# Routed experts' sums: gathered rows times diagonal matrices of the weights on TensorE, in place of one weighted addition per row on VectorE

## The reference

```python
# third block: 32 experts of inner width 96, 4 of them for each token, and a shared expert
probs = softmax(x @ router_w)
topk_w, topk_idx = top_k(probs, 4);  topk_w = topk_w / sum(topk_w)
eo[t, e] = (silu(x[t] @ w_gate[e]) * (x[t] @ w_up[e])) @ w_down[e]
routed[t] = sum over the 4 chosen e of topk_w[t, e] * eo[t, e]
out = routed + (silu(x @ sh_gate) * (x @ sh_up)) @ sh_down * sigmoid(x @ sh_gate_w)

# fourth block: 16 experts of inner width 256, 2 for each token, with biases
y[t] = sum over the 2 chosen e of gates[t, e] * ((silu(x[t] @ W1[e] + b1[e]) * (x[t] @ W11[e] + b11[e])) @ W2[e] + b2[e])
z = a shared expert of inner width 512;  out = y + z
```

## Time and profile before

| | |
|---|---|
| median of 3 runs | 1688.22 us (1686.22 to 1691.62) |
| profiled execution | 1694.55 us, its span 1692.7 us |
| PE busy | 1260.5 us (74%), 7110 instructions |
| DVE busy | 1250.0 us (74%), 4139 instructions |
| ACT busy | 910.8 us (54%) |
| POOL busy | 412.5 us (24%), 578 instructions |
| line 2151, gathers (POOL) | 96 of 977 ns mean, 93.8 us |
| granted TensorE clock, mean | 0.856 |

### The profile page before, as it was taken

How to read it: one execution, slowest core, us unless ns; L and a number is a source line. 1 busy time by engine, 2 the same in 40 slices (tenths; PEclk the granted TensorE clock), 3 DMA queues, 4 the chain that set the end, 5 groups by cost and what they waited for, 6 DMA issues and landing times.

```text
span 1692.7 us, 24051 instructions
## 1 busy us (share of the span) xinstructions
PE 1260.5 (74%) x7110; PEld 675.0 (40%) x7198; DVE 1250.0 (74%) x4139; ACT 910.8 (54%) x2172; POOL 412.5 (24%) x578
## 2 busy tenths in 40 slices
PE   6988979887422333246678999977899888999976
PEld 2444544444111111131135656513366344666621
DVE  5998979989789999868656566667766865555672
ACT  3898988887254444411344565544444444455454
POOL 0111202002000000003556345265310153232160
PEclk7999989999755555555789999978899999999998
DMA  3010100100293000012332566333211026547220
GB/s 114 26 68 8 49 27 26 55 0 1 80 330 116 3 9 11 1 39 90 114 99 83 180 186 191 100 86 67 55 32 31 35 79 159 158 123 179 98 69 21
DMA packets 141387, 135.41 MB, mean 80 GB/s; under 512 B 75218, under 2 KB 114455, under 8 KB 141203
## 3 DMA queue, kind: packets, MB, share of 16 engines
q1 hardware_dynamic: 126185, 101.99, 20.6%
q0 software_dynamic: 13440, 31.48, 6.1%
q10 hardware_dynamic: 1632, 0.39, 0.1%
HBM read 95.96 MB, written 47.27 MB: 85 GB/s over the span
## 4 chain that ended last, share of the span: by engine, by line
PE 45%; DVE 33%; ACT 9%; issue 8%; another core or an unknown queue 2%; DMA 2%; SPq 1%; POOL 0%; DVEq 0%; ACTq 0%
PE PS L577 40%; DVE RA L1733 6%; DVE nmx L1488 5%; DVE RA L1737 4%; PE PS L573 4%; DVE RA L1291 3%; DVE RA L1294 2%; ACT RA L1879 1%; ACT RA L1929 1%; DVE RB L1291 1%; DVE RB L1294 1%; DVE X L1475 1%; DVE Otok L1218 1%; ACT RB L1885 1%
## 5 line engine op out<-in xcount | busy, mean ns | idle before, releaser
L577 PE MATMUL PS<-RA 128*128 128x512 bf16 (+6 forms) x1961 | 508.3, 352 | 102.4 <-DVE nmx L1488 64.6
L1488 DVE TENSOR_REDUCE nmx<-PS 128x1 f32<-128x512 f32 x512 | 347.2, 686 | 237.2 <-PE PS L577 210.0
L1929 ACT ACTIVATE RA<-PS 128x512 f32<-128x512 f32 x512 | 301.1, 599 | 214.9 <-PE PS L577 151.4
L577 PEld LDWEIGHTS PS<-RA 128*128 128x128 bf16 (+4 forms) x2048 | 200.7, 121 | 356.3 <-issue 142.1
L577 PE MATMUL PS<-RA,Vs 128*32 128x512 f32 x1240 | 204.1, 654 | 5.1 <-ACT RA L1929 1.0
L2055 ACT ACTIVATE RA<-RA 128x8 f32<-128x8 f32 x511 | 107.5, 210 | 143.0 <-DVE RA L1733 142.7
L573 PE MATMUL PS<-ident,RB 128*128 128x128 f32 (+2 forms) x331 | 62.7, 334 | 158.5 <-DVE RB L1666 142.9
L1908 ACT ACTIVATE RA<-PS 128x256 f32<-128x256 f32 (+1 forms) x144 | 55.0, 382 | 171.7 <-PE PS L577 158.3
L1291 DVE TENSOR_SCALAR RA<-PS 128x1024 f32<-128x1024 f32 x96 | 117.0, 1219 | 20.9 <-PE PS L577 20.6
L1879 ACT ACTIVATE RA<-RA,nm 128x512 f32<-128x512 f32 x192 | 128.8, 725 | 0.9 <-POOL nm L2225 0.7
L1294 DVE CUSTOM_DVE_ANT_0 RA<-RA,RB 128x512 f32<-128x512 f32 x192 | 125.1, 689 | 3.3
(11 more groups left out here) (312 smaller groups left out, 2127.1 us busy)
## 6 DMA issues: line engine op xcount, KB each, us to landing
RA<-scr SPq DMA_DIRECT2D x288, 96.0 KB
RA<-wd SPq DMA_DIRECT2D x28, 384.0 KB
xd<-Otok SPq DMA_DIRECT2D x36, 256.0 KB, 3.3
RA<-xd POOLq DMA_DIRECT2D x72, 128.0 KB, 3.8
RA<-wd SPq DMA_DIRECT2D x56, 160.0 KB
RB<-wd SPq DMA_DIRECT2D x20, 384.0 KB
RB<-wd SPq DMA_DIRECT2D x40, 160.0 KB
scr<-parts SPq DMA_DIRECT2D x48, 128.0 KB
```

The costliest lines, as they stand in the source:

```text
L577: return e.matmul(o, l, r, start=first, stop=last)
L1488: e.tensor_reduce(nmx[:, (g + lx) % 3, c:c + 1], bank[(6, 0)[i % 2]], AX.X, ALU.max, negate=True).then_inc(*ROWMAX.up(layer, n, i))
L1929: e.activation(chunk(layer, k, i), bank[(1, 5)[i % 2]], ACT.Exp).then_inc(*EXP.up(layer, k, i))
```

## The change

`gather_steps` now lists three tasks. `gather` i goes through 8 tiles (`XY`, in the place of `XG`), and from the ninth on waits for the merge of the tile to which row i - 8 belonged. `weight` i, three steps later, is a new operation of POOL: the 128x128 identity times the column WJ[:, n, j], which gives a diagonal matrix in one of 8 tiles `DG`. `merge` n, one step after the last `weight` of the tile, is on PE: k float32 matmuls, each a diagonal matrix times a gathered tile, summed in 128 columns of bank 3 or 4, whichever of them no expert item holds (`MERGE_BANK`). DVE then adds the bank to X[n], once per token tile: 16 additions per block in place of 64 and 32. Waits that named an addition of a row name the merge or its addition. By the planner, the merges stand in quarters 194 to 257 and 477 to 508, and `READY3` becomes 208, 224, 241 and 295.

```diff
     XG = RA[:, 8448:9984].rearrange("p (u t k) -> p u t k", u=6, t=2)
+    XY = RA[:, 8448:9472].rearrange("p (u k) -> p u k", u=8)
+    DG = [x[:, i:i + 128] for x, a in ((RA, 9472), (RB, 6272)) for i in range(a, a + 512, 128)]
...
-    GATH = [loads(f"gather{i}") for i in range(6)]
+    GATH = [loads(f"gather{i}") for i in range(8)]
...
     def gather_steps(lx):
-        pairs = 16 * topk[lx]
-        return [([("combine", i - 6)] if i >= 6 else []) + ([("gather", i)] if i < pairs else []) for i in range(pairs + 6)]
+        m, pairs = topk[lx], 16 * topk[lx]
+        steps = []
+        for i in range(pairs + 4):
+            steps.append([("gather", i)] if i < pairs else [])
+            if i >= 3 and i - 3 < pairs:
+                steps[-1].append(("weight", i - 3))
+            if i >= 4 and (i - 4) % m == m - 1:
+                steps[-1].append(("merge", (i - 4) // m))
+        return steps
...
+    MERGE_BANK, held = {}, set()
+    for q in range(4 * (LEAD + STEPS)):
+        for layer, m in ((2, q // 4), (3, q // 4 - LEAD)):
+            for name, i, *_ in plan[layer].get((m, q % 4), ()):
+                if name == "hidden":
+                    held.add(3 + i % 2)
+                elif name == "gated":
+                    held.discard(3 + i % 2)
+                elif name == "merge":
+                    MERGE_BANK[layer - 2, i] = next(bk for bk in (3 + i % 2, 4 - i % 2) if bk not in held)
...
# PE
+            elif name == "merge":
+                n, m = task[1], topk[lx]
+                bk = MERGE_BANK[lx, n]
+                claim(bk)
+                for i in range(m * n, m * n + m):
+                    pe.wait_ge(GATH[i % 8], lx, i)
+                    pe.wait_ge(DIAG, lx, i)
+                    ins = mm(bank[bk][:, 0:128], DG[i % 8], XY[:, i % 8, :], i == m * n, i == m * n + m - 1)
+                ins.then_inc(*MERGE.up(lx, n))
+                free[bk] = [(XW, "routed", lx, n)]
...
# DVE
-            elif name == "combine":
-                i = task[1]
-                n, j = i // topk[lx], i % topk[lx]
-                dve.wait_ge(GATH[i % 6], lx, i)
+            elif name == "merge":
+                n = task[1]
+                dve.wait_ge(MERGE, lx, n)
                 x_last(n)
-                dve.wait_ge(ROUTE, "done", lx)
-                e.scalar_tensor_tensor(out=X[:, n, :], in0=XG[:, i % 6 // 2, i % 2, :], scalar=WJ[:, n, j:j + 1], in1=X[:, n, :],
-                                       op0=ALU.mult, op1=ALU.add).then_inc(*XW.up("routed", lx, i))
-                written[n] = ("routed", lx, i)
+                e.tensor_tensor(X[:, n, :], bank[MERGE_BANK[lx, n]][:, 0:128], X[:, n, :], ALU.add).then_inc(*XW.up("routed", lx, n))
+                written[n] = ("routed", lx, n)
...
# POOL
-                if i >= 6:
-                    pool.wait_ge(XW, "routed", lx, i - 6)
-                e.indirect_dma_start(XG[:, i % 6 // 2, i % 2, :], None, yd[lx],
-                                     bass.IndirectOffsetOnAxis(ap=IDX[:, n, j:j + 1], axis=0)).then_inc(*GATH[i % 6].up(lx, i))
+                if i >= 8:
+                    pool.wait_ge(MERGE, lx, (i - 8) // k)
+                e.indirect_dma_start(XY[:, i % 8, :], None, yd[lx],
+                                     bass.IndirectOffsetOnAxis(ap=IDX[:, n, j:j + 1], axis=0)).then_inc(*GATH[i % 8].up(lx, i))
+            elif name == "weight":
+                i = task[1]
+                n, j = i // k, i % k
+                pool.wait_ge(ROUTE, "done", lx)
+                if i >= 8:
+                    pool.wait_ge(MERGE, lx, (i - 8) // k)
+                e.tensor_scalar(DG[i % 8], ident[:, :], WJ[:, n, j:j + 1], None, ALU.mult).then_inc(*DIAG.up(lx, i))
```

More of the change, by code:

```diff
@@ L256, in build @@
     YOUT = [loads(f"yout{i}") for i in range(6)]
-    GATH = [loads(f"gather{i}") for i in range(6)]
+    GATH = [loads(f"gather{i}") for i in range(8)]
     STORE = loads("store")
     XT_P, SCORE, TURN, VALUE, MISC = (signal("pe_" + n) for n in ("xt", "score", "turn", "value", "misc"))
-    FF_P, GATE_P, HID, XTURN, DOWN = (signal("pe_" + n) for n in ("ff", "gate", "hid", "xturn", "down"))
+    FF_P, GATE_P, HID, XTURN, DOWN, MERGE = (signal("pe_" + n) for n in ("ff", "gate", "hid", "xturn", "down", "merge"))
     LN, XT_V, CLIP, ROWMAX, MISC_V, PARTS_V, FIN, XW = (signal("dve_" + n) for n in ("ln", "xt", "clip", "rowmax", "misc", "parts", "fin", "x"))
@@ L268, in build @@
     XG_A, YO_A = signal("act_xg"), signal("act_yo")
-    ROOT = signal("pool_root")
+    ROOT, DIAG = signal("pool_root"), signal("pool_diag")
     SET, PARTS_P, BIAS_P, NEGMAX = signal("pool_set"), signal("pool_parts"), signal("pool_bias"), signal("pool_negmax")
@@ L412, in build @@
     assert spread(2, gather_steps(0), last + 4, 0.95) <= 4 * STEPS
-    added = [max(4 * n + i for (n, i), tasks in plan[2].items() for t in tasks if t[0] == "combine" and t[1] // 16 == b) for b in range(4)]
+    added = [max(4 * n + i for (n, i), tasks in plan[2].items() for t in tasks if t[0] == "merge" and t[1] // 4 == b) for b in range(4)]
     READY3 = [max(added[b], 4 * (16 * b + 25) + 2, 4 * (48 + LAG) - 9) + 1 for b in range(4)]
@@ L447, in both @@
                     early_step(*task)
+    MERGE_BANK, held = {}, set()
[8 more added lines that the diff above has]
+                    MERGE_BANK[layer - 2, i] = next(bk for bk in (3 + i % 2, 4 - i % 2) if bk not in held)
+        for task in early.get(q, ()):
+            if task[:2] == ("values", 0):
+                (held.add, held.discard)[task[2] // 3](3)
     between, narrow, wide = {}, {}, {}
@@ L2165, in first_rows @@
             if lx:
-                pool.wait_ge(XW, "routed", 0, 16 * topk[0] - 1)
+                pool.wait_ge(MERGE, 0, NT - 1)
             for u in range(6):
@@ L2475, in sp_program @@
             sp.wait_ge(XW, "shared", 1, 8 * b + 7)
-            sp.wait_ge(XW, "routed", 1, 8 * b + 7)
+            sp.wait_ge(XW, "routed", 1, 4 * b + 3)
             e.dma_start(out[b].rearrange("(n p) d -> p n d", p=128), X[:, 4 * b:4 * b + 4, :]).then_inc(*STORE.up("all"))
```

## The result

The changed kernel took 1718.12 us (median of 5 runs, 1715.54 to 1723.19), the kernel before 1688.22 us (5 runs, 1684.98 to 1691.62): 1.0168 of its time, 95% interval 1.0149 to 1.0188. I had forecast 1686.0. It is slower, outside my range, and by the rival to which I had given 4 in 100: POOL is the bound.

A forecast was written before the change was run, and what follows sets the result against it. Neither PE (45% of the chain) nor DVE (33%) alone was taken to bound it. Terms -4.5 + 0.8 + 0.3 + 1.2 = -2.2 us took the median from 1688.22 to 1686.0 us; range 1676 to 1698.

The forecast's parts named there:

- POOL is the bound: Rival, both gather stretches: at 0.85 us per diagonal a pair takes 2.01 us, giving 1724; chance 0.04.
- the price of POOL's multiplication: POOL between gathers: 0.32 us per 128x128 multiplication, so 1.48 us per pair of gather and multiplication in place of 1.25.
- the room on POOL: Third block's gather stretch: about 14 us of room; POOL waits add 0.8 us there and 1.2 us in the fourth block.
- the removal of additions: DVE, both gather stretches: load falls by 17.4 and 6.4 us, worth at most PE's waits on it.
- PE's part: PE, both gather stretches: merges' matmuls add 19.0 and 10.6 us, 1.19 us per four-row merge, 0.66 per two-row merge.
- my clock return: PE, both gather stretches: denser work raises the clock; three quarters taken back, 9.2 and 2.6 us.
- PE's wait for maxima: Sign of being right: PE's wait for DVE's row maxima (nmx) under 12 us, from 19.7 and 8.0 us before.
- the clock: Sign in the gather groups: granted clock of 0.92 or more is right, still near 0.82 is wrong.
- PE is the bound: Rival, both gather stretches: added matmuls come on top, none of the clock back, +9 us, 1697; chance 0.26.
- the landing at nothing: Merges on PE waiting for the last gather's landing: costed at nothing, 4.44 us less 0.95 being enough.

The follow-up runs named there:

- e2: Changed kernel with POOL's multiplication replaced by a copy of the identity, waits kept, weights left out: 1669.12 us, ratio 1.0170 to the kernel before.
- e3: Changed kernel with the diagonal matrices made by ACT, POOL having only the gathers: 1651.90 us, ratio 1.0068 to the kernel before.
- g1: Changed kernel with POOL making a token tile's four (two) diagonals in one TENSOR_TENSOR: 1704.64 us against 1686.76, ratio 1.0100.
- h2: e3 again (changed kernel, diagonals made by ACT) in a later group of runs: 1706.32 us against 1692.86, ratio 1.0074.
- f2: The kernel before, unchanged, one execution for its trace in the group where it took 1641.25 us; gather stretches 91.1 and 33.5 us.
- f1: The changed kernel itself, run once more in another group: 1696.93 us against 1641.25 for the kernel before, ratio 1.0336.

## Why the prediction was wrong

**The failed step is the price of POOL's multiplication.** I had bounds of 0.291 us (a cast 128x128) and 0.852 us (TENSOR_TENSOR) and took 0.32, "near the cast, since both read one tensor of this size". It measured 0.63 us, and 0.31 for the copy: the cast was the right row for a copy and the wrong one for a multiplication. The gather in front of it took 1.01 us for 0.95, so the pair came to 1.84 us for 1.48. My own threshold for the POOL rival was 0.55 us per diagonal, or 1.70 us a pair; 0.63 lies above it. Between bounds that had the threshold in the middle, 4 in 100 was far too little. The forecast and the rival differed by one unmeasured number. The trace's other rows would not have settled it: of the three TENSOR_TENSOR on 18x128 one took 0.852 us and the others 0.388 and 0.417, to both sides of 0.63.
With 1.84 us in the rival's own count (64 pairs and three roots against the 112.5 us there, 32 pairs against 48.3) the stretches end 8.5 and 10.6 us later, an estimate. The two stretches grew by 27.2 us; POOL's stop in front of a root, 8.4 us, stood in no term of mine.
The Trainium skill, page "GPSIMD Engine Reference", section "Elementwise — side-by-side cycle accounting", from which I had an estimate of 0.11 us for the body, has one figure for the simplest loops and none that tells a copy from a multiplication. The runs disagree with it as a guide to the price: 0.31 and 0.57 us for the same 128 elements per partition, so a dispatch common to both can't be all of what is above the body.

**A second step is in doubt: the room on POOL.** I gave it 14 us of room over the stretch and 0.8 + 1.2 us of waits. e2, at the price I assumed, was 1.7% slower, not unchanged, and 1.0% of that is POOL's (e2 against e3). Room over a stretch is no room at each merge: the roots stand in the queue, one of them for 11.4 us from gather to gather in e2, and after that POOL has 1.44 us a pair to catch up with quarters of 91.1 / 64 = 1.42 us. But in that group the kernel before itself went from first to last gather in 95.9 us, for the 110.8 that I had reckoned with, so by my own sum (95 us and three roots) there was no room to begin with. In the slower groups g1 has nearly my price, 1.51 us a row, and is at 1.0100 where h2, with nothing on POOL, is at 1.0074: their intervals meet. So whether the room would have sufficed where I looked for it stays open. In the fourth block I had 1615 + 44.4 as "about 1658", which is 1659.4, and the last addition stands at 1663.30 us.

**What the removal of additions was worth.** I had taken 17.4 + 6.4 us off DVE's load. Its busy time fell by 76.4 - 67.7 = 8.7 and 29.8 - 26.8 = 3.0 us, half. The reason stood in the earlier trace rows: in bursts a maximum and an addition together take 0.86 us, so an addition of 0.34 us behind a maximum added only 0.17 us of busy time.

**Right: PE's part.** Eight matmuls took 1.05 us, 0.13 each (I had 1.19 us for a merge with its first loads). PE's busy time in the two stretches rose by 14.1 + 7.9 = 22.0 us; 19.0 + 10.6 less my clock return of 9.2 + 2.6 is 17.8. PE's wait for maxima is at 4.7 us, under the 12 that I had named, and that isn't only because POOL is slower still: in e3, where PE waits for no diagonal in the first stretch, it is 4.3 us, for 15.7 in f2. So the relief of DVE came. That PE's idle time was "nearly all" this wait holds for the first stretch (19.7 of 24.2 us), less for the second (8.0 of 12.0).

**Wrong: the clock.** I wanted 0.92 or more in the first stretch and counted on 9.2 us from it. It was 0.86 with PE busy 93.74 of 122.93 us, 76%. Where PE didn't wait for POOL it was higher: in e3 with PE busy 84.08 of 98.88 us, 85%, the granted clock was 0.93.
By the Trainium skill, page "TensorE: Matmul & The Clock Gate", section "What's actually happening", it is activity that releases the fast clock; these two rows agree with it.
Little of that is the merges' doing, though: the kernel before, in f2, has 0.89 in the same stretch (the first row; e3 is the second), and 1.00 in the second stretch with PE busy 27.66 of 33.52 us.

```profile
1084.87:1175.94 91.07, 72.55 (x352) 25.06 (x353) 76.27 (x216) 43.46 (x84) 61.48 (x62) 0.89 0.38 84
1084.55:1183.43 98.88, 84.08 (x462) 42.24 (x471) 65.02 (x172) 60.04 (x146) 60.16 (x62) 0.93 0.36 80
```

Even so e3 was slower than before. Its first stretch is 7.8 us longer than f2's, with PE 11.5 us more busy and 7.6 us of waits for a landing; which part of the 7.8 us is whose, and why the added matmuls don't fit into PE's idle time, wasn't tested. The rival "PE is the bound" (1697, +9 us) has the size of what is left when POOL is taken out, +0.6 to 0.7%, but not the reason, since its condition was that the clock doesn't come back.

**Wrong: the landing at nothing.** I had 4.44 us from a gather's start to its addition as enough. The landings on record in e3 lie 2.5 to 6.2 us behind the gathers' starts (see there), those of the kernel before in f2 2.5 to 7.0, and DVE waited 4.6 us in all for them in f2. In e3 a last row was met at 1148.99 us, its gather started at 1145.17. A merge stands 4 gathers behind its last row; at 1.26 us each that is 5.0 us, within that spread. In the change itself the slow POOL hid it, nearly as I had said: no such wait of PE in the first result's stretches, 1.0 us in f1 and 2.2 us of its weight loads.

## What to carry to other kernels

Between two bounds with a threshold in the middle, the operation's own price is the prediction: a row of the same engine and shape but another operation isn't it (copy 0.31 us, multiplication 0.63). Price it in a run before the forecast. Before work goes to a "free" engine, look at its period where its results are consumed in order, not at its busy share: POOL was 24% busy over the run, and in this stretch its pair of 1.84 us met quarters of 1.62. Undo one part at a time in one group of runs, with a neutral edit beside them: where the change cost 3.4%, 2.7% went when POOL's work did, and the 0.7% left fell to 0.2% with later merges; what in these 0.2% is PE's work and what DVE's relief lies within the 0.4% that a neutral edit showed. A single trace of the change showed only the first.

## What the runs showed of the hardware

On POOL, a 128x128 f32 multiplication by a column takes 0.63 us, by a constant 0.57, a copy 0.31; a TENSOR_TENSOR that makes 128x512 takes 1.05 us, 0.26 per 128 columns. The same diagonal takes 0.40 us on ACT, and four of them 0.68 us on DVE.

The kernel before ran in 1641 us in some groups and in 1687 to 1693 in others, at a granted clock of 0.86 to 0.87 in both. The slower kind has pauses with the work at hand, as far as the modelled ends of PE's matmuls tell, that the profile puts down to an unknown queue or to "issue"; in the profile of the first result the kernel before has 91 us of such waits on ACT and DVE ("remote"), f2 has none, and the spans differ by 53.7 us. One of them, in h2: PE made two tiles of scores from 1141.75 to 1142.35 us; ACT's next instruction started 2.9 us and DVE's 4.4 us later:

```profile
1141.75 0.60 PE L600 MATMUL PS<-RA 125*128 125x512 bf16 x2
...
1145.29 0.60 ACT L1852 ACTIVATE QK<-PS 128x512 f32<-128x512 f32 x1 [4.04 <-issue]
...
1146.72 0.69 DVE L1518 TENSOR_REDUCE nmx<-PS 128x1 f32<-128x512 f32 x1 [6.26 <-remote]
```

The changed kernel has 41.8 us of "remote" waits in the first result and none in f1, with spans 16.6 us apart. That would follow if such a pause cost less where POOL is the bound, and it would fit the 1.7% of the first result against 3.4% in f1; it wasn't tested. What these pauses are, and what parts the two kinds of groups, wasn't found.

An indirect gather of 128 rows of 512 bytes starts every 1.26 us when nothing stands between two (0.95 us and 0.30 us until the next), every 1.44 us with a copy between and every 1.84 us with the multiplication.
